# Third block of a four-block cross-attention kernel: v, y and the norm's rows in other slots, and the first heads' mask products ahead of the MLP's last sums

## What is computed

```python
def block3(hidden, enc, ltor_mask, cross_mask, ...):
    ln_out = layernorm(hidden, ln1_s, ln1_b)
    q, k, v = split(ln_out @ w_qkv + b_qkv)
    ctx = merge_heads(attention(split_heads(q), split_heads(k), split_heads(v), ltor_mask))
    x = hidden + ctx @ w_ao + b_ao
    ln_out = layernorm(x, ln2_s, ln2_b)
    q = ln_out @ w_q + b_q
    k, v = split(enc @ w_kv + b_kv)
    x = x + merge_heads(attention(split_heads(q), split_heads(k), split_heads(v), cross_mask)) @ w_co + b_co
    ln_out = layernorm(x, ln3_s, ln3_b)
    return x + gelu(ln_out @ w1 + b1) @ w2 + b2

def attention(q, k, v, mask):                      # 16 heads of 16
    scores = (q @ k.T) / 4
    scores = scores * mask - 10000.0 * (1.0 - mask)
    return softmax(scores) @ v
```

## Time and profile before

| | us |
|---|---|
| median of three runs | 1579.45 (1579.08 to 1579.54) |
| profiled execution, device time | 1580.77 |
| profiled execution, first to last instruction (span) | 1578.8 |
| PE, DVE, ACT, POOL busy | 1487.7, 935.2, 905.5, 145.1 |
| TensorE clock granted, mean | 0.98 of full |

### The profile page before, as it was taken

One profiled execution on the slowest core, in us unless ns is written; L12 is line 12 of the kernel. 1 busy time (PEld: TensorE's weight loads), 2 busy tenths in 40 slices (PEclk: granted clock), 3 DMA queues, 4 the chain that ended last, 5 costly groups with the idle time before them and its releaser, 6 DMA issues.

```text
span 1578.8 us, 28651 instructions
## 1 busy us (share of the span) xinstructions
PE 1487.7 (94%) x9824; PEld 1146.0 (73%) x9824; DVE 935.2 (59%) x3314; ACT 905.5 (57%) x2807; POOL 145.1 (9%) x163
## 2 busy tenths in 40 slices
PE   7999999999999999999999999997898788999996
PEld 5766687788787787778788777785666566866664
DVE  4777623455554455445455455326988995168897
ACT  5788834444443444444444444435888786379996
POOL 2010010000000000000000000111222221022200
PEclk9999999999999999999999999998899999999999
DMA  7000103010010101001010000001000000000000
GB/s 288 2 2 2 63 1 120 1 47 15 8 54 1 62 1 48 15 1 61 1 47 16 1 1 1 1 1 54 1 2 17 26 14 8 1 1 8 15 8 15
DMA packets 10878, 40.64 MB, mean 26 GB/s; under 512 B 2416, under 2 KB 2672, under 8 KB 8688
## 3 DMA queue, kind: packets, MB, share of 16 engines
q1 hardware_dynamic: 10736, 38.82, 6.8%
HBM read 37.77 MB, written 1.05 MB: 25 GB/s over the span
## 4 chain that ended last, share of the span: by engine, by line
PE 69%; ACT 11%; DVE 8%; issue 3%; DVEq 0%; POOLq 0%; POOL 0%; ACTq 0%
PE bank L772 7%; PE bank L753 7%; PE bank L786 7%; PE bank L745 7%; PE bank L732 7%; PE bank L735 7%; ACT probs L943 7%; PE bank L712 5%; PE bank L701 5%; PE bank L761 4%; PE bank L558 4%; DVE probs L1186 3%; ACT pT L951 2%; PE bank L580 2%; PE bank L545 2%
## 5 line engine op out<-in xcount | busy, mean ns | idle before, releaser
L943 ACT ACTIVATE probs<-probs,negmax 128x256 f32<-128x256 f32 (+1 forms) x640 | 347.8, 555 | 59.6 <-DVE negmax L1186 59.2
L1017 ACT ACTIVATE pT<-bank 128x512 f32<-128x512 f32 x128 | 76.4, 597 | 387.8 <-PE bank L761 387.8
L558 PEld LDWEIGHTS bank<-ident,probs 128*128 128x128 f32 x1536 | 177.9, 146 | 103.9 <-issue 49.5
L558 PE MATMUL bank<-ident,probs 128*128 128x128 f32 x1536 | 234.0, 289 | 17.6 <-ACT pT L951 13.1
L1318 DVE TENSOR_REDUCE stats<-bank 128x1 f32<-128x257 f32 x256 | 108.4, 425 | 212.4 <-PE bank L753 211.4
L1186 DVE CUSTOM_DVE_ANT_0 probs<-bank,mask_a 128x256 f32<-128x256 f32 (+1 forms) x384 | 174.0, 508 | 29.9 <-PE bank L545 25.5
L951 ACT ACTIVATE pT<-bank 128x512 f32<-128x512 f32 x288 | 170.2, 592 | 29.4 <-PE bank L558 29.1
L772 PE MATMUL bank<-pT,probs 128*128 128x256 f32 x512 | 132.7, 381 | 2.7 <-ACT pT L1017 2.7
L753 PE MATMUL bank<-kT,pT 128*128 128x257 f32 x512 | 132.7, 382 | 0.6 <-ACT pT L1000 0.6
L943 ACT ACTIVATION_READ_ACCUMULATOR probs<-probs,negmax 128x1 f32 x640 | 129.9, 203 | 0.0
L545 PE MATMUL bank<-kT,q_res 32*128 32x256 f32 (+1 forms) x1280 | 112.0, 456 | 15.6 <-DVE negmax L1186 8.4
(11 more groups left out here) (110 smaller groups left out, 2488.5 us busy)
## 6 DMA issues: line engine op xcount, KB each, us to landing
w_m<-in_w SPq DMA_DIRECT2D x6, 1024.0 KB, 7.5
g_qkv<-in_g SPq DMA_DIRECT2D x4, 1536.0 KB, 6.5
q_res<-in_g SPq DMA_DIRECT2D x4, 1536.0 KB, 6.3
w_qkv<-in_w SPq DMA_DIRECT2D x3, 768.0 KB, 4.4
g_bv<-in_gbv SPq DMA_DIRECT2D x8, 256.0 KB, 6.6
g_o<-in_go SPq DMA_DIRECT2D x4, 512.0 KB, 3.3
q_res<-in_go SPq DMA_DIRECT2D x4, 512.0 KB, 3.4
rows<-in_rows SPq DMA_DIRECT2D x1, 1664.0 KB, 13.9
```

The lines of the kernel that those rows point to most:

```text
L558: last = nc.tensor.transpose(out[:, n * P:(n + 1) * P], probs[:, u % PROBS, q * T + t * P:q * T + (t + 1) * P], ident[:, :])
L943: last = nc.scalar.activation(s, s, ACT.Exp, bias=negmax[:, u % PROBS, k:k + 1], scale=-1.0, accum_out=sums[:, tile % 2, q, j * c.res + r: ...
```

## The change

Three things are changed. In the third block v is projected in slots 9 and 10 instead of 13 and 14, and y in slots 11 and 12 instead of 10 and 11; the norm's rows are turned in slot 1 instead of 0, since `norm_slot` follows `y_slot`. `row_stats` and `norm_rows` of the last batch ahead of the block move into DVE's slots 4 and 9, and its turn from slot 10 of the first part to slot 1 of the second; POOL takes the power in its slot 6. And the sums of the last batch of m1 and m2 (`mlp_sums`) are done by DVE inside the attention that follows: in block 3 behind the first four mask products, in block 4 behind the first two maxima.

```diff
--- before.py
+++ after.py
@@ -120,7 +120,7 @@
         return self.pv_slot((tile + 1) * self.tile_vqs - 1)
 
     def y_slot(self, p):
-        return self.tile_slot(2 * p + 1) + 4
+        return self.tile_slot(2 * p + 1) + (5 if self.kinds == "mult" else 4)
 
     def norm_slot(self, p):
 
@@ -147,12 +147,12 @@
 
 
         p, s = divmod(slot, self.units)
-        at = [3, 6, 13] if self.kinds == "mult" else [2, 6, 14] if len(self.loads()) == 3 else [2, 6, 14, 22, 26]
+        at = [3, 6, 9] if self.kinds == "mult" else [2, 6, 14] if len(self.loads()) == 3 else [2, 6, 14, 22, 26]
         return [(n, p + 1) for n, x in zip(self.loads(), at) if x == s and p + 1 < len(self.parts)]
 
     def normed(self, slot):
 
-        got = [-1] if slot == 10 and self.host else []
+        got = [-1] if self.host and slot == (self.norm_slot(-1) if self.kinds == "mult" else 10) else []
         return got + [p for p, x in enumerate(self.parts) if x.norm != "l3" and self.norm_slot(p) == slot]
 
     def _bank_uses(self):
@@ -1110,6 +1110,16 @@
                     last = v.tensor_scalar(hT[:, b, k, :], src[:, k * T:(k + 1) * T], col(scale, k), None, ALU.mult)
                 last.then_inc(sem("l_hv"), 1)
 
+            def mlp_sums(n, b):
+                st = S[f"m{n}"]
+                added(dve, f"m{n}", b)
+                dve.wait_ge(sem("m_y"), st.at("m_y", b, 1))
+                for q in range(QT):
+                    xq = x_rows[:, b * QT + q, :]
+                    last = v.tensor_tensor(xq, bank[4 + q][:, 0:D], xq, ALU.add)
+                last.then_inc(sem("m_out"), 1)
+                dve.wait_ge(sem("m_out"), st.at("m_out", b, 1))
+
             def projections_of(c):
 
                 st = S["a" + c.name]
@@ -1243,16 +1253,21 @@
                         if what[0] == "v":
                             values(what, 0)
                 if c.kinds == "mult":
-                    times_mask(0)
+                    for u in range(QUAD):
+                        times_mask(u)
+                    mlp_sums(1, B - 1)
                 for slot in range(c.last_slot() + 1):
                     if slot < c.count:
                         maxima(slot)
-                        if c.kinds == "mult" and slot < 3:
-                            times_mask(slot + 1)
-                        elif c.kinds == "mult" and slot % QUAD == 3 and slot + 1 < c.count:
+                        if c.kinds == "mult" and slot % QUAD == 3 and slot + 1 < c.count:
                             for u in range(slot + 1, slot + 1 + QUAD):
                                 times_mask(u)
-                    if slot == 3 and c.host:
+
+                    if c.name == "3" and slot == 1:
+                        mlp_sums(2, B - 1)
+                    if c.name == "2" and slot == 4:
+                        row_stats(c.host, B - 1, x_rows)
+                    if c.name == "2" and slot == 9:
                         norm_rows(c.host, B - 1, x_rows)
                     if c.host and c.kinds == "add":
                         if slot % QUAD == 3:
@@ -1279,6 +1294,7 @@
                                 values(what, p)
 
             def mlp(n, before, own, queries=None, values=None):
+
                 st = S[f"m{n}"]
                 if n == 1:
                     norm_rows(before, B - 1, x_rows)
@@ -1288,15 +1304,10 @@
                     if b == B - 1 and queries:
                         queries(0)
                         values("v0", 0)
-                    added(dve, f"m{n}", b)
-                    dve.wait_ge(sem("m_y"), st.at("m_y", b, 1))
-                    for q in range(QT):
-                        xq = x_rows[:, b * QT + q, :]
-                        last = v.tensor_tensor(xq, bank[4 + q][:, 0:D], xq, ALU.add)
-                    last.then_inc(sem("m_out"), 1)
-                    if NORMS[own][0] != "raw":
-                        dve.wait_ge(sem("m_out"), st.at("m_out", b, 1))
-                        row_stats(own, b, x_rows)
+                    if b < B - 1 or not queries:
+                        mlp_sums(n, b)
+                        if NORMS[own][0] != "raw":
+                            row_stats(own, b, x_rows)
 
             def wide(j, before, own):
                 st = S[f"b1{j}"]
@@ -1503,6 +1514,8 @@
 
             def after2(slot):
                 c = SMALL[1]
+                if slot == 6:
+                    power("l21", B - 1)
                 if slot == 12:
                     pool.wait_ge(sem("l_z"), S["l21"].at("l_z", 0, B))
                     bias("o2s", B - 1)
@@ -1535,8 +1548,6 @@
             additive(SMALL[1], "2", 0)
             for b in range(B - 1):
                 power_and_bias("l21", b, "o2s")
-
-            power("l21", B - 1)
             attention(SMALL[1], after2)
             for b in range(B - 1):
                 pool.wait_ge(sem("l_t"), S["l3t"].at("l_t", 0, b + 1))
```

## The result

The changed kernel takes 1601.54 us (median of four runs, 1597.99 to 1604.38) against 1579.49 (1579.08 to 1580.07): a ratio of 1.0141, 95% interval 1.0129 to 1.0154. The forecast had the direction, and the wait on which it rested is there, but the time lies above the range (1592.0, 1579 to 1598). The profiled run took 1601.59 us; its span is 1599.8, 21.0 more than before's 1578.8.

A forecast was written before the change was run, and what follows sets the result against it. No engine full in the third block, DVE nearest, held up by PE's 3.1 us wait for v. Terms -1.7 + 11.2 - 1.2 + 6.0 - 1.8 = +12.5 on the profiled 1580.77 gave 1593.3, median 1592.0 us; range 1579 to 1598.

The forecast's parts named there:

- ACT's order: Third block: rows leave bank 7 behind unit 16's exponentials, so q and slot 4's scores wait; a part takes 31.1 us at full clock.
- D: Steady parts of the third block: the end of DVE's maximum of slot 0 of the next part, from which waits are counted.
- At the lower clock q takes 1.66 and the scores 2.09: Third block's parts: PE's idle gap before q lowers the clock, 1.8 us more, 32.9 a part.
- That v is projected earlier costs nothing: Third block's parts: PE has k's copy by then, and DVE reaches slot 9's end when PE has just finished v.
- a wait of 0.55: Third block's parts: DVE waits while PE does half of y and slot 12's scores, replacing 0.56 for y; stretch stays 27.0 to 27.1.
- Up to 1076 us ... the change touches nothing there: Before the third block's attention: PE is busy 1052.30 of 1076.00 us at full clock; no time change was counted.
- m2's first batch: y's moved half stands directly ahead of the turn of its normed rows: +4.1 for the wait, +1.9 for the clock, +6.0.
- Head: Third block's head, up to slot 4's products in the second part: earlier products gain, -1.7 (at full clock -3.5).
- Seventh and eighth part: Third block's end: no q follows the seventh, 29.6 instead of 30.14; the eighth loses its wait for y; -1.2 together.
- Fourth block: Its head: the first two maxima no longer wait for the sums, so exponentials start at 1391.36 instead of 1393.24; -1.8.
- The weight load of q: Third block: pulled ahead it would save 0.2 us a part, but the trace showed it waiting 2.8 us, so nothing was counted.
- the low clock lasts: Rival: 6 us of low clock instead of 3.9 after each gap, 1 us more for ACT in six places: 1598, chance 0.15.

The follow-up runs named there:

- short filler: Changed kernel plus unused products on PE in the third block, four ahead of the turn and six ahead of q: 1590.44 us, 1.0064.
- second profile: The changed kernel profiled once more, no edit: 1604.53 us (1602.99 to 1604.61).
- the kernels of the table: Kernels with single slots or heads put back or moved; those at 28.5 to 28.7 us a part have v in 12 or y in 11, turn in 0: 1560.1 to 1569.4 us.
- e4_rows_first: Changed kernel with ACT taking the norm's rows out of bank 7 ahead of the exponentials of unit 16 instead of behind them: 1580.25 us, 1.0013.
- e12_y_alone: Kernel before with the change's order at the heads of blocks three and four and y one slot later (11); v in 13, turn in 0: 1560.1 us.

## Why the forecast was wrong

The mechanism was right, and two terms of the sum were too small: a part was put at 32.9 us and took 33.9, through waits of DVE that the forecast priced at nothing or too low (third point), and the unchanged code was put at 0 and lost 3.6 us (fourth point). The seventh and eighth part and m2 took about a microsecond more each than forecast, and the head 2.2 less.

- **"ACT's order"**, D + 4.0 or D + 5.8: right. In the changed kernel it is D + 5.86 in the mean of the five parts, with the short filler D + 4.39 (1237.37 to 1241.76 us). Swapping ACT's two steps takes 11.45 us out of the five parts.
- **"At the lower clock q takes 1.66 and the scores 2.09"**: right in kind. Measured with the filler it is 1.65 us a part by the first profile and 2.2 by the second, forecast 1.8. That q's gap would start it fits three of the five parts of the first profile; in the other two PE is slow before it comes to q's wait, behind the 1.93 us before the turn, which I passed over with "that gap matters little". q's wait is 2.7 to 3.5 us, not 4.3.
- **"That v is projected earlier costs nothing", "a wait of 0.55"**: this step failed. DVE waits 0.46 for v and 0.90 for the scores of slot 12, since PE has to wait 0.54 for v's copy before y. With 0.56 for y gone, the stretch to D is 27.9 (1209.50 to 1237.37 us with the filler) and not 27.1. In the changed kernel itself it is 28.0 in the mean of the five parts, with the low clock's tail at slot 8. Together with the 0.39 behind D this is the 1.15 us by which 32.25 exceeds 31.1. With 1.65 instead of 1.8 for the clock a part comes to 33.9 instead of 32.9, and five of them to +16.2 instead of +11.2: 5.0 of the 8.5 us that the sum was short. In the second profile it is 7.6 of 11.4, and there the clock has a share in it.
- **"Up to 1076 us ... the change touches nothing there"**: true of the code, and 3.6 us in the profile (2.1 in the second). I had put this term at nothing; the clock in unchanged code differed.
- **m2's first batch**, +6.0: mechanism right, 7.2 measured and 7.24 given back by one edit; the low clock cost 3.1 instead of 1.9, near the upper bound of 7.1 for the term.
- **Head**, -1.7: the clock held there (q 1.13 us behind a gap of 2.71), so it was -3.9, near the full-clock value of -3.5; in the second profile it did not hold (q 2.08 us behind a gap of 2.72), and it was -2.0. **Seventh and eighth part**, -1.2: -0.1, the waits for v and slot 12 again. **Fourth block**, -1.8: -2.0.
- The weight load of q, for which the forecast names a wait of 2.8 us in the earlier trace rows, waited twice there, 2.8 us in all and 1.4 at the longest; no term hung on it.
- The range ended at 1598, where only the clock's duration was stretched. All terms of the steady part had been taken at my best estimate, and nothing in the range stood for a wait that the old trace doesn't show. The rival "the low clock lasts" came nearest with 1598, but for another reason: it asks for 2.8 us of clock a part, and by the short filler the whole of the clock is 1.65 to 2.2, about the 1.8 of the forecast itself.

The Trainium skill (TensorE: Matmul & The Clock Gate, Why this matters for your kernels) says to leave no long idle gaps between bursts of matmuls. The rows without and with filler agree with it (33.9 and 32.25 us), and the kernels of the table show its better use (28.5 to 28.7 us): the gap was closed by ordering, not by filling.

## What to carry to other kernels

When a step moves by one slot on one engine, look up where its consumer stands on the *next* engine's list: here one place on ACT put a 1 us copy behind a maximum that comes 3 us later; undoing it took 11 us out of five parts and 21 off the median. Before several steps are moved, move each by itself: of this change's five parts, in the order of the table, two are worth 9 and 11 us, and three cost 4, 12 and 25. And a result in a bank blocks the bank's next user; writing it earlier helps only if its reader is earlier too.

## What was not expected of the hardware

- Behind gaps of 0.7 to 1.1 us on PE the granted clock is low in some runs and not in others, in code that is the same (two places, 0.59 and 0.63 against 1.00), and which ones goes with how early the clock rose at the start of the run.
- The fall comes late: in the changed kernel the turn and four transposes behind the gap of 1.93 us still take 0.63 and 0.60 us, and the slow stretch begins a microsecond later (two of five parts) or at q, behind its own wait (three). What it costs depends on which instructions it meets: 30.35 or 32.31 us for a part of e4_rows_first.
- One half of DVE's maximum takes 1.49 us instead of 0.42 when it meets POOL's addition to x_rows (1205.79 us above), once per part, as it did before the change (1.47 to 1.49). POOL at that time:

```profile
1205.61 1.39 POOL L1442 TENSOR_TENSOR x_rows<-x_rows,rows 128x512 f32<-128x512 f32 x1 [2.07 <-DVE y_rows L1099]
```

The Trainium skill (SBUF — State Buffer, SBUF: two separate sides) says that the two share a pair of ports, and that one of them stands for a whole instruction of the other where DVE reads two inputs from SBUF, as this maximum does (probs, mask_a). The trace agrees: the half maximum starts 0.18 us into POOL's 1.39 and ends 0.28 behind it. In e12_y_alone, where DVE reads v out of PSUM at the start of that addition, the same maximum takes 0.93 us. That is 0.5 us a part there, where DVE is the busiest engine (27.6 of 28.7 us), and 1.1 in the changed kernel; moving it was not tried.
